# Guess moves without their middle state, and a new order of small work, in a recurrent layer

## Reference

```python
def rms(z):
    return z / jnp.sqrt(jnp.mean(z * z, axis=-1, keepdims=True) + EPS)

def polar_orthogonal(W, iters=12):
    X = W / (jnp.linalg.norm(W) + 1e-08)
    # 12 times: X = 1.5 * X - 0.5 * (X @ X.T @ X)

xn = layernorm(x)                         # x: (8, 512, 128), float32
O_lh, O_rh = polar_orthogonal(W_lh), polar_orthogonal(W_rh)
q, v = xn @ Wq.T, xn @ Wv.T
h = identity                              # then, for each of the 512 times t:
h = rms(h @ O_lh.T + q_t @ O_rh.T);  qs_t = h
attn = (qs * v) @ Wc.T
ffn = sqrt((xn @ cos(theta + theta_noise))**2 + (xn @ sin(phi + phi_noise))**2)
out = x + attn + ffn
```

## Time and profile before

| | us |
|---|---|
| median of 3 runs | 133.49 |
| the runs | 133.40 to 133.55 |
| the profiled execution | 133.2 |
| its span | 131.3 |
| TensorE busy | 112.1 |
| VectorE busy | 85.1 |
| ScalarE busy | 75.1 |
| GpSimd busy | 68.4 |

### The profile page before, as it was taken

The page is one execution under the profiler, slowest core; times in us unless marked ns, Lnnn a source line. Parts: engine busy times, 40 slices in busy tenths (PEclk is TensorE's granted clock), DMA queues, the critical chain, the costliest instruction groups (busy, mean ns, idle before and its releaser), DMA issues.

```text
span 131.3 us, 2507 instructions
## 1 busy us (share of the span) xinstructions
PE 112.1 (85%) x665; PEld 87.2 (66%) x665; DVE 85.1 (65%) x358; ACT 75.1 (57%) x283; POOL 68.4 (52%) x112
## 2 busy tenths in 40 slices
PE   6999999999868796989886969999999999987610
PEld 6888788878846474778664747676776666765300
DVE  3447777767666654555656647888788778878720
ACT  4164557585256574566846566766776776655100
POOL 6335889882367218011422225588888678874200
PEclk9999999999999999999999999999999999999985
DMA  4983000000000000000000000022020202202110
GB/s 105 282 309 124 2 0 7 0 0 5 0 0 0 0 0 2 0 0 5 0 0 0 0 0 5 5 82 77 3 80 0 80 0 82 79 8 80 40 45 10
DMA packets 3346, 4.98 MB, mean 38 GB/s; under 512 B 448, under 2 KB 1344, under 8 KB 3328
## 3 DMA queue, kind: packets, MB, share of 16 engines
q1 hardware_dynamic: 3024, 4.46, 9.9%
q0 software_dynamic: 160, 0.26, 0.6%
q10 hardware_dynamic: 144, 0.07, 0.2%
HBM read 2.69 MB, written 2.10 MB: 36 GB/s over the span
## 4 chain that ended last, share of the span: by engine, by line
PE 68%; DVE 17%; ACT 6%; issue 4%; DVEq 1%; ACTq 0%
PE bank L956 10%; PE bank L939 10%; PE bank L974 8%; PE bank L847 5%; PE bank L864 5%; PE bank L919 5%; DVE W L702 4%; PE bank L866 4%; PE bank L947 4%; PE bank L975 3%; DVE SQM L690 3%; DVE WMID L685 3%; PE bank L992 3%; DVE bank L696 2%; PE bank L805 2%
## 5 line engine op out<-in xcount | busy, mean ns | idle before, releaser
L302 POOL TENSOR_SCALAR XN<-X,MV,RSTD 128x128 f32<-128x128 f32 x32 | 25.6, 812 | 15.3 <-DVE RSTD L577 15.3
L309 POOL TENSOR_TENSOR FS<-FSQ 128x256 f32<-128x256 f32 x16 | 11.6, 727 | 13.5 <-ACT FSQ L460 13.5
L939 PE MATMUL bank<-CS,XNT 128*128 128x256 f32 x64 | 16.5, 380 | 0.0
L685 DVE SCALAR_TENSOR_TENSOR WMID<-UZ,RT,bank 128x129 f32<-128x129 f32 x29 | 10.1, 349 | 8.7 <-PE bank L974 4.3
L919 PE MATMUL bank<-IDENT,W 128*128 128x128 f32 x29 | 9.4, 323 | 7.4 <-DVE W L702 7.3
L956 PE MATMUL bank<-WCT,PV 128*128 128x128 f32 x64 | 14.8, 312 | 0.5 <-DVE OUT L720 0.4
L974 PE MATMUL bank<-PXT,WT 128*128 128x128 f32 x58 | 14.0, 323 | 1.2 <-DVE WT L669 1.1
L441 ACT ACTIVATE SQE<-W 128x129 f32<-128x129 f32 x30 | 9.4, 313 | 9.7 <-DVE W L702 9.7
L314 POOL TENSOR_TENSOR XF<-X,FR 128x256 f32<-128x256 f32 x16 | 11.6, 726 | 5.6 <-ACT FR L467 5.6
L919 PEld LDWEIGHTS bank<-IDENT,W 128*128 128x128 f32 x29 | 4.0, 139 | 14.7 <-DVE W L702 14.6
L669 DVE COPY WT<-bank 128x128 f32<-128x128 f32 x28 | 8.1, 291 | 8.5 <-PE bank L919 8.5
(11 more groups left out here) (169 smaller groups left out, 267.9 us busy)
## 6 DMA issues: line engine op xcount, KB each, us to landing
X<-in_L_attn_x_dram SPq DMA_DIRECT2D x8, 256.0 KB, 5.4
out_dram<-OUT SPq DMA_DIRECT2D x7, 256.0 KB, 2.0
out_dram<-OUT SPq DMA_DIRECT2D x2, 128.0 KB, 1.7
WP<-in_L_attn_W_rh_dram ACTq DMA_DIRECT2D x1, 64.0 KB, 2.0
WP<-in_L_attn_W_lh_dram SPq DMA_DIRECT2D x1, 64.0 KB, 2.2
ANG<-in_L_ffn_theta_dram POOLq DMA_DIRECT2D x1, 64.0 KB, 3.5
WV<-in_L_attn_Wv_dram SPq DMA_DIRECT2D x1, 64.0 KB, 3.3
ANG<-in_L_ffn_phi_dram POOLq DMA_DIRECT2D x1, 64.0 KB, 3.2
```

The costliest lines, as they stand in the source:

```text
L302: pool.tensor_scalar(XN[:, t, :], X[:, t, :], MV[:, t, 0:1], RSTD[:, t:t + 1], ALU.subtract, ALU.mult).then_inc(S["xn_done"], 1)
L309: pool.tensor_tensor(FS[:, f % 2, :, :], FSQ[:, f % 2, :, 0:P], FSQ[:, f % 2, :, P:2 * P], ALU.add).then_inc(S["ffn_sum"], 1)
L685: dve.scalar_tensor_tensor(out=WMID[:, 0:E], in0=UZ[:, uz(j), 0:E], scalar=norm_of(m), in1=YB[:, 0:E], op0=ALU.mult, op1=ALU.add).then_inc ...
L939: last = pe.matmul(FB[:, i * 2 * P:(i + 1) * 2 * P], XNT[:, tile(2 * f + i)], CS[:, :], start=True, stop=True)
```

## The change

In a guess move WMID is no longer made. The mean square of the middle state u*n + y (u entry, n norm, y = YB) is put together from three terms. n*n*mean(u*u) is GROWN, on VectorE, from SSU (`entry_squared`) and the sum of squares of W. mean(y*y) is SSY, a Square with accumulator on ScalarE. The cross term 2n*mean(u*y) is CROSS, on VectorE: since y = W.O, u.y equals W.(u.O'), so that UZ gets a fourth part, u.O' scaled by 2/C, which a third part of MNT makes and which doesn't need y. ScalarE's root takes SSY as input and CROSS as bias. Move 0 takes the state from ROWS in PSUM.

Further: a pair is four parts wide, in `pair` and in both copies. ScalarE copies pair m+1 in each move m, right after the root of the middle, instead of behind the root of W. Pair m+2 is made in move m, in front of the tiles, and pairs 1 and 2 both in move 0. Tiles come one move pair earlier (tile 2 behind the M products, tile 3 behind pair 0). FFN products 0 to 2 are in moves 8, 10, 12. A V product follows the transpose in every move; 14 and 15 are in moves 8 and 9. Of the last two V copies one is done by VectorE in move 10. `rows_prepared` on VectorE stands behind `end`. In polar, NEXTT of matrix 1 is issued between the next iteration's GRAM of matrix 0 and of matrix 1. SHIFTED and E0COL are made at VectorE's start, `place_h0` is called in iteration 0 instead of 3, and the angles' steps in 5, 7, 9 and 11 instead of 7 to 10.

```diff
     def uz(j):
-        return (j // 2) * 3 + (2 if j % 2 else 0)
+        return (j // 2) * 4 + (3 if j % 2 else 0)
...
-    PAIRS_A = {**{m: (m + 1,) for m in range(9)}, 9: (10, 11), **{m: (m + 2,) for m in range(10, 14)}}
-    TILES_A = {0: 3, 2: 4, 4: 5, 6: 6, 8: 7}
-    FFN_A = {7: 0, 8: 1, 11: 2, **{m: m - 11 for m in range(GUESSES, GUESSES + 13)}}
-    V_A = {1: (0,), 3: (3,), 7: (7,), 13: (13, 14, 15)}
-    V_B = {1: 1, 2: 2, 4: 4, 5: 5, 6: 6, 8: 8, 9: 9, 10: 10, 11: 11, 12: 12}
-    V_COPIED = {1: (0,), 3: (1,), 5: (2,), 7: (3,), 9: (4,), 11: (5,), 13: (6, 7)}
+    PAIRS_A = {m: (m + 2,) for m in range(14)}
+    TILES_A = {0: 4, 2: 5, 4: 6, 6: 7}
+    FFN_A = {8: 0, 10: 1, 12: 2, **{m: m - 11 for m in range(GUESSES, GUESSES + 13)}}
+    V7_COPIED = 10
+    V_A = {8: (14,), 9: (15,)}
+    V_B = {m: m for m in range(14)}
+    V_COPIED = {1: (0,), 3: (1,), 5: (2,), 7: (3,), 9: (4,), 11: (5,), 13: (6,)}
...
             act.copy(MNT[:, 1, :], GRAM[1][:, 0:P]).then_inc(S["nt_copied"], 1)
+            act.wait_ge(S["g_done"], 1)
+            act.activation(MNT[:, 2, :], GRAM[0][:, 0:P], ACT.Copy, scale=2.0 / C).then_inc(S["nt_copied"], 1)
             deviations(5)
+            xt_copied(2)
...
                 act.wait_ge(S["uz_copied"], i)
-                act.copy(UZ[:, uz(2 * q):uz(2 * q) + 3, 0:P],
-                         PJ[i % 2][:, 0:3 * P].rearrange("p (a c) -> p a c", a=3)).then_inc(S["uz_copied"], 1)
+                act.copy(UZ[:, uz(2 * q):uz(2 * q) + 4, 0:P],
+                         PJ[i % 2][:, :].rearrange("p (a c) -> p a c", a=4)).then_inc(S["uz_copied"], 1)
...
             norm_of_state(0)
+            xt_copied(3)
...
                 if m < GUESSES:
-                    act.wait_ge(ssm_ready, m + 1)
+                    act.wait_ge(y1_done, m + 1)
+                    act.activation(SQY[:, :], YB[:, 0:P], ACT.Square, scale=1.0 / math.sqrt(C),
+                                   accum_out=SSY[:, 0:1]).then_inc(ssy_ready, 1)
+                    act.wait_ge(ssy_ready, m + 1)
+                    act.wait_ge(cross_ready, m + 1)
+                    act.activation(RT[:, j:j + 1], SSY[:, 0:1], ACT.Sqrt, bias=CROSS[:, 0:1]).then_inc(rm_ready, 1)
                 else:
-                    act.wait_ge(mid_ready, m + 1)
+                    act.wait_ge(mid_ready, m - GUESSES + 1)
                     act.activation(SQM[:, 0:E], WMID[:, 0:E], ACT.Square, accum_out=SSM[:, 0:1]).then_inc(ssm_ready, 1)
-                    act.wait_ge(ssm_ready, m + 1)
-                act.activation(RT[:, j:j + 1], SSM[:, 0:1], ACT.Sqrt, scale=1.0 / C).then_inc(rm_ready, 1)
+                    act.wait_ge(ssm_ready, m - GUESSES + 1)
+                    act.activation(RT[:, j:j + 1], SSM[:, 0:1], ACT.Sqrt, scale=1.0 / C).then_inc(rm_ready, 1)
+                if m + 1 < len(PAIRS):
+                    pair_copied(m + 1)
...
                     xt_copied(TILES_A[m])
-                for i in PAIRS_A.get(m, ()):
-                    pair_copied(i)
...
                                   ALU.add, ALU.mult).then_inc(S["h0_placed"], 1)
-
-            def place_shift():
-
-                dve.memset(SHIFTED[:, :], 0.0).then_inc(S["shift_placed"], 1)
-                dve.wait_ge(S["shift_placed"], 1)
-                dve.tensor_copy(split(SHIFTED[:, :])[:, :, 1:NCHUNK],
-                                ends(IDENT[:, :])).then_inc(S["shift_placed"], 1)
-
-            def place_e0():
-                dve.tensor_reduce(E0COL[:, :], split(IDENT[:, :])[:, :, 0], mybir.AxisListType.X,
-                                  ALU.add).then_inc(S["e0_placed"], 1)
...
                     row_stats(it // 2, back)
-                if it == 3:
+                if it == 0:
                     place_h0()
-                if it == 5:
-                    place_shift()
-                    place_e0()
-                if it == 7:
-                    turns_off(0, TWO_PI_A)
-                if it == 8:
-                    turns_off(1, TWO_PI_B)
-                if it == 9:
-                    turns_off(2, TWO_PI_C)
-                if it == 10:
+                if it in (5, 7, 9):
+                    turns_off(it // 2 - 2, (TWO_PI_A, TWO_PI_B, TWO_PI_C)[it // 2 - 2])
+                if it == 11:
...
-            def mid_norm(m):
-                dve.wait_ge(mid_ready, m + 1)
-                dve.tensor_tensor_reduce(out=SQM[:, 0:E], in0=WMID[:, 0:E], in1=WMID[:, 0:E], scale=1.0,
-                                         scalar=0.0, op0=ALU.mult, op1=ALU.add,
-                                         accum_out=SSM[:, 0:1]).then_inc(ssm_ready, 1)
+            def grown(m, j):
+
+                dve.wait_ge(ss_ready, m + 1)
+                dve.wait_ge(ssu_ready, m + 1)
+                dve.tensor_scalar(GROWN[:, :], SSU[:, j // 2:j // 2 + 1], SSE[:, m % 2:m % 2 + 1], 1.0 / C,
+                                  ALU.mult, ALU.mult).then_inc(grown_ready, 1)
+
+            def cross(m, j):
+
+                dve.wait_ge(S["uz_copied"], m + 1)
+                dve.wait_ge(r_ready, m + 1)
+                dve.wait_ge(grown_ready, m + 1)
+                if m == 0:
+                    dve.wait_ge(S["rows_done"], 1)
+                dve.tensor_tensor_reduce(out=SQM[:, 0:P], in0=W[:, 0:P] if m else ROWS, in1=UZ[:, uz(j) + 2, 0:P],
+                                         scale=norm_of(m), scalar=GROWN[:, 0:1], op0=ALU.mult, op1=ALU.add,
+                                         accum_out=CROSS[:, 0:1]).then_inc(cross_ready, 1)
+
+            def entry_squared(m, j):
+
+                dve.wait_ge(S["eps_ready"], 3)
+                dve.wait_ge(S["uz_copied"], m + 1)
+                dve.tensor_tensor_reduce(out=SQU[:, 0:E], in0=UZ[:, uz(j), 0:E], in1=UZ[:, uz(j), 0:E],
+                                         scale=1.0 / C, scalar=0.0, op0=ALU.mult, op1=ALU.add,
+                                         accum_out=SSU[:, j // 2:j // 2 + 1]).then_inc(ssu_ready, 1)
...
             dve.wait_ge(S["uz_done"], 1)
-            dve.tensor_copy(UZ[:, uz(2 * PAIRS[0]):uz(2 * PAIRS[0]) + 3, 0:P],
-                            PJ[0][:, 0:3 * P].rearrange("p (a c) -> p a c", a=3)).then_inc(S["uz_copied"], 1)
+            dve.tensor_copy(UZ[:, uz(2 * PAIRS[0]):uz(2 * PAIRS[0]) + 4, 0:P],
+                            PJ[0][:, :].rearrange("p (a c) -> p a c", a=4)).then_inc(S["uz_copied"], 1)
...
                 j = MOVES[m][0]
-                rows_prepared(m)
+                entry_squared(m, j)
+                grown(m, j)
+                cross(m, j)
...
                     end_prepared(m)
-                mid(m, j)
-                mid_norm(m)
...
                 end(m, j)
+                rows_prepared(m)
+                if m == V7_COPIED:
+                    dve.wait_ge(S["v7_done"], 2)
+                    dve.tensor_copy(VT[:, (BATCHES - 1) * BANK:], VB[BATCHES - 1][:, :]).then_inc(S["v7_copied"], 1)
...
+            def next_transposed(it, m):
+                pe.matmul(NEXTT[m][:, 0:P], PP[m][:, :], PXT[it % 2][m][:, :], start=True,
+                          stop=True).then_inc(S["nextt_done"], 1)
+
...
                         pe.wait_ge(S["px_copied"], it * 2 + m - 1)
+                        if m:
+                            next_transposed(it - 1, 1)
...
                     transpose_tiles(1)
-                if it == 11:
-                    transpose_tiles(2)
...
                                   stop=True).then_inc(S["next_done"], 1)
-                        pe.matmul(NEXTT[m][:, 0:P], PP[m][:, :], PXT[it % 2][m][:, :], start=True,
-                                  stop=True).then_inc(S["nextt_done"], 1)
+                        if m == 0:
+                            next_transposed(it, 0)
...
             pe.matmul(GRAM[0][:, 0:P], WQ[:, :], OT[1][:, :], start=True, stop=True).then_inc(S["mt_done"], 1)
+            transpose_tiles(2)
...
             pe.matmul(NEXT[1][:, 0:P], OL[:, :], OT[0][:, :], start=True, stop=True).then_inc(S["o2_done"], 1)
+            pe.wait_ge(S["mt_copied"], 1)
+            pe.matmul(GRAM[0][:, 0:P], M[:, :], OL[:, :], start=True, stop=True).then_inc(S["g_done"], 1)
...
                     pe.wait_ge(S["uz_copied"], i - 1)
-                pe.wait_ge(S["nt_copied"], 1)
+                pe.wait_ge(S["nt_copied"], 2)
                 b = PJ[i % 2]
-                pe.matmul(b[:, 0:2 * P], XNT[:, tile(2 * q)], MNT[:, :, :].rearrange("p a c -> p (a c)"),
+                pe.matmul(b[:, 0:3 * P], XNT[:, tile(2 * q)], MNT[:, :, :].rearrange("p a c -> p (a c)"),
                           start=True, stop=True)
-                pe.matmul(b[:, 2 * P:3 * P], XNT[:, tile(2 * q + 1)], MNT[:, 0, :], start=True,
+                pe.matmul(b[:, 3 * P:4 * P], XNT[:, tile(2 * q + 1)], MNT[:, 0, :], start=True,
...
             pair(0)
+            transpose_tiles(3)
...
                 pe.matmul(PB[:, 0:P], stationary(m), O2T[:, :], start=True, stop=True).then_inc(y2_done, 1)
+                if m == 0:
```

(38 more changed lines are left out.)

5 lines of the change are left out of this document (1 added, 4 removed).

## The result

The changed kernel takes 138.8 us (median of 4 runs, 138.3 to 139.27) beside 133.52 for the kernel before (133.4 to 133.76): a ratio of 1.039, 95% interval 1.035 to 1.043. I had forecast 132.2, with 130.6 to 134.0 as the range. It is slower by 5.3 us, and the forecast is wrong in sign.

The account below looks back on a forecast made before the run. The prediction took the guess moves as a waiting chain and polar as one dependent chain, with TensorE full in the sure moves. Terms: +2.3 - 0.25 + 0.7 - 3.7 - 0.6 + 0.3 = -1.25 us, from 133.49 to 132.2, range 130.6 to 134.0.

Parts of the forecast that it names:

- Polar: Polar loop: NEXTT of matrix 1 fills the gap before GRAM 1, GRAM 0 starts 0.03 earlier; -0.25 us, bounds 0 and -1.3.
- H: Polar start: VectorE waits for H's load in iteration 0, delaying PP of iteration 1 to 10.2; +2.3 us, bounds +1.5 and +2.8.
- rival 3: Polar: TensorE's clock falls in the gap while waiting on H, slowing iterations; total 133.1 to 134, chance 0.10.
- Guess moves: Moves 1 to 13: without the middle state an undisturbed move takes 2.46 us, 0.31 less; together 35.1 for 38.8, -3.7 us.
- a slack of 0.1: Guess move: CROSS ready 0.8 to 0.9 us after the product, ScalarE's root wanting it at 0.93.
- rival 2: Guess moves: VectorE's new chain ends last, by port or slower handovers, and W waits; 134.2 us, chance 0.19.
- the 0.25 that I had added for the V copies: Six odd guess moves: the V copy behind W's root can delay the next Square by 0.04; +0.25 us.
- Port: Guess moves: GpSimd sums and adds meet SQU or CROSS about five times, 0.2 us each; +0.3 us.
- the half that came from the rule: Moves 0 to 6: SQU and CROSS each wait out a GpSimd operation in about half of them, cancelling the gain there.
- Move 13: Last guess move: keeps its seam, with VectorE's DIAG and V product 13 added in the way; 3.4 us.
- the entry: Move 0: wider pair and tile 3 in TensorE's queue put the next product at 37.9 instead of 37.2; +0.7 us.
- The seam: Into the sure moves: one V copy goes to VectorE in move 10, so TensorE's wait there goes; -0.6 us.

## Why the prediction was wrong, by its own steps

**Polar: the step that failed first.** I wrote that NEXTT "fills the gap before GRAM 1" and put it at -0.25, with bounds of 0 and -1.3. In the diff it stands behind the wait for `px_copied`, and at m = 1 that is PX of matrix 1. It does not fill the gap, it begins where the gap ends, and delays GRAM of matrix 1 by its own 0.22 us. The loop of matrix 1 closes over it: 16.64 - 14.64 = 2.00 us against 1.83. That is +0.17 in a steady iteration. The two in which TensorE transposes tiles behind this GRAM, of which I had written that they "gain nothing", lose more, 0.40 and 0.28 (2.35 and 2.23 for 1.95). From PP of iteration 1 to PP of iteration 11 it is 20.09 us for 18.52, and 0.3 more behind it make the +1.9 of the profile; alone the edit measured +2.1. The error was one of reading, a line above or below a wait. My bounds left out a loss altogether, though the queue's order was there to read. With the line above the wait, the -0.25 would have been about right (0.28 in the profile) and too small for the whole time to show.

**H: mechanism and size right.** The wait, the queue behind it and the order of the chain came as written: +2.3 forecast, PP of iteration 1 at 10.2 forecast and 10.71 seen. The difference is H's landing, 6.2 us after issue instead of 5.5, less 0.2 for the three operations, which took 0.47 us where I had 0.66 with the handover. Alone the edit measured +2.0 by its ratio. Undone in the changed kernel it gave 2.9, of which 1.0 is the clock, a term of its own.

**The clock (rival 3).** Its price, 0.9 to 1.8 us on the forecast, held (1.2 to 1.4 in polar, 1.0 at the seam); its chance did not. I gave it 0.10, and four of five profiled executions with the wait show a fall, three of them in polar. It should have stood with the H term, as part of it. The changed kernel's own fall came at the seam, a place that I had not named.

**Guess moves: the term that was mis-sized.** -3.7 for moves 1 to 13; measured 37.88 us (43.08 to 80.96) instead of 38.78, so -0.9. The forecast of ScalarE's side was right: Square at +0.52, the root 0.29 long, and once CROSS is no longer late, the root at +0.92 and moves 3, 5 and 7 of 2.44 against my 2.46. VectorE's chain was the error. I had CROSS ready at 0.8 to 0.9. The rows give: SQU at -0.14 and its sum at +0.15 as forecast, GROWN at +0.26 and not right behind it, 0.21 long, then 0.17 of idle between GROWN and CROSS, where I had 0.07, so CROSS from +0.65 and not +0.45, 0.41 long and not 0.35: ready at +1.06. In place of a slack of 0.1 the root came 0.23 late. That is rival 2's place, by handovers and not by port. The rival had 0.19, and its own reason ("handovers of 0.16 where others are 0.03") was the one that came about. Seven moves at 2.68 instead of 2.46 are 1.5 us, less the 0.25 that I had added for the V copies. Moves 8, 10 and 12 with FFN were close (3.37, 2.94 and 2.94 for 3.31 and twice 2.88).

**Port.** +0.3 in the sum. Move 9 alone took 3.20 and move 11 2.89. The rows of SQU, and of the GpSimd sum in move 9:

```profile
L718 DVE CUSTOM_DVE_ANT_0 SQU<-UZ x14: 284/285/806, 40.2 to 77.0; 128x129 f32<-128x129 f32 x14
```

```profile
64.98 0.73 POOL L318 TENSOR_TENSOR FS<-FSQ 128x256 f32<-128x256 f32 x1 [8.64 <-ACT FSQ L474]
65.05 0.81 DVE L718 CUSTOM_DVE_ANT_0 SQU<-UZ 128x129 f32<-128x129 f32 x1
```

SQU began 0.07 after the GpSimd sum and ended 0.15 after it. In moves 11 and 13 SQU took 0.40 instead of 0.28 and CROSS 0.50 and 0.51 instead of 0.41, each beside a GpSimd addition and each ending 0.15 after it. So the term was about 1.0 us (0.52 in move 9, 0.22 in each of moves 11 and 13), because the stretched operations are now on the path of the root. With SQU early, move 9 got 0.69 back (0.24 of it the gain of any such move), but the CROSS of move 13 took 0.85 beside a GpSimd addition. The Trainium skill (SBUF — State Buffer, section "SBUF: two separate sides") has a GpSimd operation that reads SBUF and a VectorE operation with two SBUF inputs excluding each other for a whole instruction. The trace agrees for the GpSimd additions, by the rows above. It does not for the row normalisation: in move 5 SQU took 0.28 and CROSS 0.41 us, their usual times, inside 3.13 us of GpSimd's XN, and SQU stayed at 0.28 to 0.29 in all of moves 1 to 6, each time beside it. Here the measurement decides, and half of rival 2, the half that came from the rule, is refuted.

**Move 13 and the entry.** Move 13: 3.4 forecast, 3.81 measured; its root waited 0.48 us for CROSS, and DIAG stands behind that. From the last product of polar to the second guess product: +1.2 us (0.8 to the first, 0.37 in move 0) for +0.7. The seam gave 0.47 of the 0.6 where the clock held (2.99 for 3.46; the move behind it is 0.08 longer).

Without the order of polar and the wait for H, these are -0.9 - 0.5 + 1.2 = -0.2 us, and +0.2 with the 0.4 of move 22 (last section). The ratio measured for this remainder is 1.0015, +0.2 us. In the forecast it was -3.7 - 0.6 + 0.7 + 0.3 = -3.3.

The forecast was 6.6 us too low. By size that is the guess moves with the port 2.5 (-3.4 forecast, -0.9 measured), the order of polar 2.3, the clock at the seam 1.0, the entry 0.5, move 22 0.4 and the seam 0.1, less 0.3 for H. These are readings of single profiled executions, good to a few tenths.

## What to carry to other kernels

When an instruction moves in a queue, read the waits between its old and its new place, and write down for the instructions behind it which loop they close; a product a line below a wait cost 2.1 us, a line above it cost nothing. When work leaves one engine for another, sum the new engine's chain from measured durations of the nearest form and a handover for every dependent pair, even on the same engine, and ask which operand was ready long ago: moving the sum of squares into an earlier wait (with the row work out of the way) turned a change worth nothing into one worth 2 us. And a load without hurry becomes urgent when its first user moves: issuing H first was worth 3.2 us, 1.0 of it in the clock.
